# Summed features through memory, and 32 KB of scratch for the gathers

## What is computed

```
e = stack([tbl_f[ids[:, f]] for f in range(39)], axis=1)      # 2048 x 39 x 16
xk = e
for idx, (W, b) in enumerate(((w0, b0), (w1, b1), (w2, b2))):
    z = relu(einsum('bhd,bkd,hks->bsd', e, xk, W) + b)         # 128 rows s
    # layers 0 and 1: the first 64 rows go on as xk, the last 64 are direct output; layer 2: all 128
h = concat([sum over d of the 256 direct rows, dense_ctx], axis=1)
y = relu(relu(h @ W_top1 + b_top1) @ W_top2 + b_top2) @ W_top3
```

## Time and profile before

| | |
|---|---|
| median of 3 runs | 2478.45 us (2478.34 to 2480.01) |
| the profiled execution | 2477.58 us |
| its span | 2475.8 us, so 1.8 us lie around it |
| busy share of the span | PE 98%, PEld 66%, DVE 89%, ACT 70%, POOL 79% |
| DMA | 352.6 MB, mean 142 GB/s, mean busy share of the 16 engines 67% |

### The profile page before, as it was taken

How to read it: one execution, slowest core, us unless ns; L and a number is a source line. 1 busy time by engine, 2 the same in 40 slices (tenths; PEclk the granted TensorE clock), 3 DMA queues, 4 the chain that set the end, 5 groups by cost and what they waited for, 6 DMA issues and landing times.

```text
span 2475.8 us, 33269 instructions
## 1 busy us (share of the span) xinstructions
PE 2422.1 (98%) x8854; PEld 1640.9 (66%) x8854; DVE 2211.2 (89%) x1876; ACT 1724.4 (70%) x2185; POOL 1948.6 (79%) x1331
## 2 busy tenths in 40 slices
PE   5999999999999999999999999999999999999989
PEld 2566666666666666666666666666666666666655
DVE  1599999999989999999999999899999999999990
ACT  1677777777767777767777776676777777677663
POOL 6688888888878888888888888788888888865550
PEclk9899999999999999999999999999999999999999
DMA  3778667766856766776686677577668667766830
GB/s 74 157 145 175 141 138 160 158 137 141 175 124 139 174 134 140 163 157 137 144 172 138 139 161 160 121 157 160 137 139 174 145 139 154 164 136 134 171 84 0
DMA packets 214716, 352.60 MB, mean 142 GB/s; under 512 B 34382, under 2 KB 47566, under 8 KB 214588
## 3 DMA queue, kind: packets, MB, share of 16 engines
q1 hardware_dynamic: 194717, 347.07, 65.4%
q0 software_dynamic: 19968, 5.15, 2.1%
HBM read 346.97 MB, written 5.12 MB: 142 GB/s over the span
## 4 chain that ended last, share of the span: by engine, by line
PE 54%; POOL 26%; issue 14%; DVE 4%; ACT 1%; POOLq 0%; DMA 0%; ACTq 0%; DVEq 0%
PE ps L858 20%; POOL Pl L397 11%; POOL emb L391 11%; PE ps L868 11%; PE ps L848 10%; PE ps L836 8%; PE ps L831 2%; POOL dir L426 2%; DVE P L731 1%; DVE ps L731 1%; DVE Pl L736 1%; PE ps L983 1%; POOL sqx L403 1%; PE ps L975 1%; PE ps L824 1%
## 5 line engine op out<-in xcount | busy, mean ns | idle before, releaser
L397 POOL TENSOR_TENSOR Pl<-P,Ph 128x1024 fp32r<-128x1024 f32 x448 | 1074.8, 2399 | 285.3 <-ACT Ph L541 261.5
L858 PE MATMUL ps<-Ph,wh 128*128 128x512 f32 x2048 | 965.2, 471 | 9.9 <-ACT Ph L541 9.9
L541 ACT ACTIVATE Ph<-ps 128x1024 fp32r<-128x1024 f32 x576 | 590.3, 1025 | 406.7 <-DVE ps L731 393.0
L731 DVE TENSOR_TENSOR P<-xb,ps 128x1024 f32<-128x1024 f32 x704 | 853.2, 1212 | 2.8 <-DMA xb<-x_dram 2.8
L736 DVE TENSOR_TENSOR Pl<-ps,Ph 128x1024 fp32r<-128x1024 f32 x576 | 705.1, 1224 | 116.1 <-ACT Ph L541 97.4
L858 PE MATMUL ps<-Ph,wl 128*128 128x512 f32 x1920 | 755.5, 393 | 0.0
L868 PE MATMUL ps<-Pl,wh 128*128 128x512 f32 x2048 | 742.2, 443 | 7.4 <-POOL Pl L397 7.4
L391 POOL DMA_INDIRECT emb<-tbl_in,idx x624 | 600.6, 962 | 170.5 <-issue 145.0
L731 DVE TENSOR_TENSOR ps<-xb,ps 128x1024 f32<-128x1024 f32 x576 | 707.1, 1228 | 28.5 <-issue 9.4
L541 ACT ACTIVATE Ph<-P 128x1024 fp32r<-128x1024 f32 x448 | 473.9, 1058 | 186.1 <-DVE P L731 129.8
L868 PEld LDWEIGHTS ps<-Pl,wh 128*128 128x128 f32 x2048 | 384.3, 188 | 200.0 <-issue 118.2
(11 more groups left out here) (68 smaller groups left out, 857.2 us busy)
## 6 DMA issues: line engine op xcount, KB each, us to landing
xb<-x_dram SPq DMA_DIRECT2D x1280, 256.0 KB
emb<-tbl_in,idx POOLq DMA_INDIRECT x624
x_dram<-rows SPq DMA_DIRECT2D x64, 78.0 KB
xb<-w_in SPq DMA_DIRECT2D x16, 128.0 KB
xb<-wt_in SPq DMA_DIRECT2D x2, 512.0 KB, 4.4
xb<-dense_in SPq DMA_DIRECT2D x1, 768.0 KB, 5.3
wp<-w_in SPq DMA_DIRECT2D x4, 128.0 KB
xb<-w0a_in SPq DMA_DIRECT2D x1, 448.0 KB
```

Of the source, the lines that this page charges most:

```text
L397: pool.tensor_tensor(Pl[:, h_slot(ref, c, k)], P[:, p_slot(ref, c, k)], Ph[:, h_slot(ref, c, k)], ALU.subtract).then_inc(low_pool, 1)
L541: act.activation(Ph[:, h_slot(ref, c, k)], p, ACT.Copy).then_inc(rounded, 1)
L731: dve.tensor_tensor(p, xb[:, x], xk.unsqueeze(1).broadcast_to([128, 2, N]), ALU.mult)\
L858: pe.matmul(z_of(c, k), w[:, q, j, :], Ph[:, h_slot(ref, c, k), j, :], start=k in (L1B, L2) and i + j == 0, stop=False)
```

## The change

`feat` shrinks to one tile, 128 x 2 x 128 numbers. SP stores it to a tensor in memory once per tile, at the start of chunk 1 of the next tile, and POOL's last fold of a tile first waits until the store before it has landed. At the end SP loads the features back, block by block, into parts of `xb` that are free by then, and ACT and DVE wait for these loads. The one row of results moves from `xb` to `dir0`. SP's tile 0 is written out ahead of its loop. And the scratch for the descriptors of POOL's DMAs is set to 32768 bytes per partition.

```
+STORE_AT = 1
...
-        feat = sb("feat", [128, 2, BATCH])
+        feat = sb("feat", [128, 2, TB])
...
-        y_sb = xt[0:1, 12:16, :].rearrange("p t n -> p (t n)")
+        y_sb = dir0[0:1, :, :].rearrange("p t n -> p (t n)")
+        FEAT_SLOTS = (3, 0, 2, 6)
...
         def feat_block(s):
-            return feat[:, :, s * N:(s + 1) * N]
+            return xb[:, FEAT_SLOTS[s]]
...
-            def tile(T, ref, last=False):
+            def store_feat(T):
+                sp.wait_ge(folds0, FOLDS * (T + 1))
+                sp.wait_ge(folds1, FOLDS * (T + 1))
+                sp.dma_start(feat_dram[:, :, bass.ds(T * TB, TB)], feat[:, :, :]).then_inc(feat_out, 16)
+
+            def load_feat(s):
+                sp.dma_start(xb[:, FEAT_SLOTS[s]], feat_dram[:, :, s * N:(s + 1) * N]).then_inc(feat_in[s], 16)
+
+            def tile(T, ref, first=False, last=False):
                 for c in range(CPT):
+                    if c == STORE_AT and not first:
+                        store_feat(T - 1)
...
-            with sp.Fori(0, TILES - 1) as T:
+            tile(0, 0, first=True)
+            with sp.Fori(1, TILES - 1) as T:
                 tile(T, 1)
...
+            sp.wait_ge(feat_out, 16 * (TILES - 1))
+            load_feat(0)
+            sp.wait_ge(mlp_low, 3)
+            load_feat(1)
+            load_feat(2)
             sp.wait_ge(products, STEP[CHUNKS - 1, L2 + 1])
             sp.dma_start(dense_st, dense_d).then_inc(dense_in, 16)
+            store_feat(TILES - 1)
+            sp.wait_ge(feat_out, 16 * TILES)
+            load_feat(3)
...
                 if stage:
                     pool.wait_ge(done, FOLDS * T + stage)
+                if stage == FOLDS - 1 and col == 0 and not start:
+                    pool.wait_ge(feat_out, 16 * T)
...
-                    o_ = feat[:, col, bass.ds(T * TB, TB)]
+                    o_ = feat[:, col, :]
...
             def round_feat(s):
-                tiles = (s + 1) * N // TB
-                act.wait_ge(folds0, FOLDS * tiles)
-                act.wait_ge(folds1, FOLDS * tiles)
+                act.wait_ge(feat_in[s], 16)
...
             def low_feat(s):
                 dve.wait_ge(split_done, ring_left(s))
+                dve.wait_ge(feat_in[s], 16)
...
-    nc = bacc.Bacc("TRN2", target_bir_lowering=False, num_devices=1)
+    nc = bacc.Bacc("TRN2", target_bir_lowering=False, num_devices=1, dynamic_dma_scratch_size=32768)
```

More of the change, by code:

```diff
@@ L130, in fills, with build @@
     return 2 * T + c // 2 + 1 if p < PRE else CPT * T + c + 1
-def build(nc, ids, tables, x0_dram, sel0_d, inc_d, w0a_d, w0b_d, w1_d, w2_d, b_d, dense_d, wt1_d, wx_d, bt1_d, wt2_d, bt2_d,
+def build(nc, ids, tables, x0_dram, feat_dram, sel0_d, inc_d, w0a_d, w0b_d, w1_d, w2_d, b_d, dense_d, wt1_d, wx_d, bt1_d, wt2_d, bt2_d,
           wt3_d, out):
@@ L259, in build @@
         folds1 = sem("folds1")
+        feat_out = sem("feat_out")
+        feat_in = [sem(f"feat_in_{s}") for s in range(4)]
         dense_in = sem("dense_in")
@@ L409, in low_emb, with fold @@
                                    ALU.subtract).then_inc(emb_low, 1)
-            def fold(buf, col, done, T, stage, last, half):
+            def fold(buf, col, done, T, stage, last, half, start=False):
                 if stage:
                     pool.wait_ge(done, FOLDS * T + stage)
+                if stage == FOLDS - 1 and col == 0 and not start:
+                    pool.wait_ge(feat_out, 16 * T)
                 if stage == 0:
@@ L423, in fold, with fold0 @@
                 else:
-                    o_ = feat[:, col, bass.ds(T * TB, TB)]
+                    o_ = feat[:, col, :]
                     x, y = buf[:, last, N // 2:N // 2 + TB], buf[:, last, N // 2 + TB:]
                 pool.tensor_tensor(o_, x, y, ALU.add).then_inc(done, 1)
-            def fold0(T, stage):
-                fold(dir0, 0, folds0, T, stage, 3, 2)
+            def fold0(T, stage, start=False):
+                fold(dir0, 0, folds0, T, stage, 3, 2, start)
             def fold1(T, stage):
@@ L484, in tile @@
                                 pool.wait_ge(z1_read, T * CPT + CPT)
-                            fold0(T, FOLD0_AT.index(k) + 1)
+                            fold0(T, FOLD0_AT.index(k) + 1, first)
                         if c == 1 and k == LOW_AT and not last:
@@ L1050 @@
     x0_dram = nc.dram_tensor("x0_dram", (SCRATCH, NF, N), F32, kind="Internal").ap()
-    build(nc, ap["ids"], [ap[f"tbl_{f}"] for f in range(NF)], x0_dram, *[ap[k] for k in names[1:]], out)
+    feat_dram = nc.dram_tensor("feat_dram", (128, 2, BATCH), F32, kind="Internal").ap()
+    build(nc, ap["ids"], [ap[f"tbl_{f}"] for f in range(NF)], x0_dram, feat_dram, *[ap[k] for k in names[1:]], out)
     return run_bass_kernel_spmd(nc, [{f"{k}_in": v for k, v in arrays.items()}], core_ids=[0]).results[0]["y_out"]
```

## The result

The change makes the kernel slower. Over 8 runs each, the median is 2485.78 us (2484.46 to 2487.28) against 2479.15 us before (2477.45 to 2481.21). The ratio is 1.003 with a 95% interval of 1.0021 to 1.0038. The forecast was 2486.7 us. The profiled execution has a span of 2485.5 us against 2475.8. These two differ by 9.7 us and the medians by 6.6, since the profiled execution is the slowest of the eight for the changed kernel, and that of the kernel before lies near the fastest of its own.

What follows compares the result with a forecast made beforehand. PE, busy 98% of the span, was taken to bound the kernel. From 2477.58 us, minus 11.6 for the old waits, plus 20.7 for the new, came 2486.7 us; range 2469.5 to 2491.5, the forecast's own 2482 to 2491.5.

Steps and rivals of the forecast that it cites:

- The larger scratch removes the five waits of 113: POOL's idle times in front of gathers, one each 113 gathers, all go: minus 11.6 us.
- The lap becomes 128: POOL would wait behind 128, 256, 384 and 512 gathers, a supposed second limit; new waits 20.7 us, chance 0.66.
- rival 1: Bytes alone count: POOL waits behind 227 and 454 gathers, first price 5.5 us, second 0; 2471.5 us, chance 0.17.
- 2 (113): The scratch is not what fills: all POOL's waits stay, 2477.6 us; chance 0.08 together with rival 4.
- 3 (another lap): Another count between 113 and 227, two to five POOL waits at 0 to 9.4 us each: 2466 to 2490, chance 0.09.
- the upper bound of 227: Most gathers between two POOL waits with the larger scratch, twice 113 if bytes alone count: 226 or 227.
- The three prices: Cost of POOL's new waits behind 128, 256 and 384 gathers: 9.4, 5.8 and 5.5 us.
- Behind 512 nothing: POOL's wait at the gather at 1783.04, DMA engines at a share of 0.04 shortly before: price 0, at most 0.5 us.
- which costs nothing if none is under way: POOL's wait at a full lap lasts until all issued gathers have landed, so it is free with none under way.
- The store, the tail and the start: SP's store per tile, block 3's store and load at the end, first 39 gathers: price 0, tail up to 1 us.
- rival 4: Block 3's store and load take 5 us longer, ACT and PE wait: up to 3 us; chance 0.08 with rival 2 (113).
- The line of prices: PE's cost for a POOL delay: zero up to 2.5 us, then up to 1.2 us for each us above 4.

Runs made afterwards that it cites:

- The kernels in which the waits cost next to nothing: Kernel before at 11264 bytes with three spare gathers (own or common semaphore), kernel after with six on the common semaphore: 2466.39, 2465.92, 2465.69 us.
- the run with small gathers: Kernel after (32768 bytes) with a second gather of 64 rows ahead of each of the first 39, into an unread buffer; 2535.94 us in a single run.
- the run with three spare gathers: Kernel before at 11264 bytes with three more gathers into an unread buffer behind the first 57, on their own semaphore; 2466.39 us, ratio 0.9955.
- the run with 117: Kernel before with its scratch set to 16896 bytes, so that POOL stops after each 117 gathers; 2484.43 us, ratio 1.003.

## Why the prediction was right, and where its steps were off

**The larger scratch removes the five waits of 113.** Right: no wait is left at these places, and the waits are worth what was said. The kernels in which the waits cost next to nothing stand at 2465.7 to 2466.4 us, against 2477.58 - 11.6 = 2466.0.

**The lap becomes 128.** Right, but it was a supposition, and the chance of 0.66 rested on nothing that a row showed. That the number is just 128 was luck, and the whole sum hangs on it. The run with 24 KB shows that a second limit stands there, and the run with small gathers that it does not count rows. Rivals 1 (227), 2 (113) and 3 (another lap) fell with it. The 16 KB of the kernel before, from which rival 1 and the upper bound of 227 take their "twice", stand in no row of before. The run with 16384 bytes written out shows them, by its waits behind the same 113, 226, 452 and 565 gathers. Below the second limit the lap does go by the bytes: from the 113, 5696, 11264 and 16896 bytes should give 39.3, 77.7 and 116.5, and the runs have 39, 78 and 117. These three laps say nothing of the limit of 128.

**The three prices.** Forecast 9.4, 5.8 and 5.5 us, measured 10.0, 6.0 and 4.8. The sum is 20.8 for 20.7, since the errors cancel, which is luck too. The forecast started from the profiled execution of before and so gave 9.1 us more than it. The profiled executions differ by 9.7 us, the medians by 6.6. The delays were 8.78, 6.05 and 4.99 us for a forecast of 8.4, 5.4 and 5.1. So the steps from the DMA engines' share to the landing and from there to POOL were good to 0.65 us, 0.3 of it because clearing 128 takes 3.0 and not 2.7. The size of the pieces was less right: PE idled 7.77 us behind the first for "about 6", and worked at the half clock for 3.7 us, not 5.4 as behind the earlier trace rows. In the kernel before, half of those 5.4 us at a granted share of 0.50, 2.7 us, and the 4.16 us of the earlier trace rows make up the 6.8 us of the tile. No run shows the 0.7 us by which the delay behind 384 is raised from 4.4 to 5.1 for the store. The delay came out at 4.99 us there with 32 KB, and at 4.5 us with 24 KB and the same store.

**Behind 512 nothing.** Right in time, for an incomplete reason. I had said that nothing was under way, and that such a wait is free. The runs with laps of 39, 78 and 117 show that it isn't: an empty wait still costs 23.3 ns for each gather of the lap, 3.0 us with 128. It was free behind 512, and behind 339 before, because a fold or a low part was running on POOL in the meantime. The step that failed is the clause "which costs nothing if none is under way". It stood in the prediction unharmed, as none of its four places was an empty one without cover. It failed openly in the runs with 11264 bytes, which were expected at 2466.9 us and came out at 2478.

**The store, the tail and the start.** Right. The kernel after with 16384 bytes is at 1.0003 of the kernel before, the path from the last fold to block 3 took 7.0 us for a forecast of 7 to 8, and ACT's slack of 1.80 us is untouched, so rival 4 fell. Only SP's wait was mis-sized. No run shows the 0.6 to 1.2 us that the store was to add to it: it is 0.3 us longer in the chunk of the store, and as much in the chunk ahead, which has none. It costs nothing either way, as that ratio shows.

**The line of prices.** In the kernel after it held to 0.7 us, for delays of 5 us and more. It is not one line, for two reasons. POOL's lead belongs to the place: 1 us of delay cost 0.7 to 0.9 us at a tile's first gather, and 2.5 us cost nothing where the waits of the run with three spare gathers fell. And the clock takes its part or not: with 24 KB the third wait, a delay of 4.5 us, cost 2.6 us with PE's clock in full, where the kernel after paid 4.8 for a delay of 5.0 with the clock at half, and the run with 117 has both prices, 2.7 and 4.2 us, for one delay of 2.85 us.

## What to carry to other kernels

Where an engine idles in front of a DMA that waits for nothing in the program, count the DMAs between such places: the constant counts here, 113 with 16 KB and 128 with 24 and 32 KB, were the mark of a limit, and its length decided where in the schedule the stops fell. The larger scratch did not remove them. It only put four stops of 128, three of them at worse places, in place of five of 113. Shifting the count by a few gathers, so that the stops fell where POOL's lead or a long instruction covered them, took nearly all of their cost away, also with a scratch smaller than that of before. Price a stop by what is still under way, plus the clearing (23.3 ns for each gather of the lap here), less what runs on that engine in the meantime, and read the cover at that place.

## What the hardware showed that was not expected

- A stop at the end of a lap costs 23.3 ns for each gather of the lap even when all landed over 20 us ago: 1.83, 2.75 and 3.65 us of idle time at 39, 78 and 117, of which 0.8 us are there without a stop. It runs beside an instruction that is still at work on POOL: 0.21 us of idle time at a lap of 78 behind a low part of 2.4 us, in place of 2.75.
- Above a scratch of some 18,400 bytes more of it should bring nothing (an estimate: 128 gathers of 143.7 to 144.4 bytes each, as 16384 bytes held 113 and not 114, and 16896 held 117): 24 and 32 KB both stop at 128 DMAs, and a DMA of 64 rows counts like one of 128 (89 + 39 = 128 up to the first long wait).
- The count starts again when the gathers' semaphore changes: 191 = 63 + 128 and 138 = 60 + 78 with a second semaphore, 128 and 78 with one. What the chip or its runtime does at such a change wasn't tested further. Whether the first of the two changes starts it as well can't be told here, since the second follows three or six gathers later.
- The same idle time of PE, 2.3 us behind the same work, was followed by PE's clock in full at two places of the run with laps of 117, and by 3.4 us at half of it at the other three (0.65 on average in the window shown). The tiles took 2.7 and 4.2 us more.
- Behind the last landing POOL needed 3.0 us with 128 gathers in the kernel after, but with 113 in the kernel before 2.6 to 2.7 us at two places and 2.1 us at two others.
